# Linear attention on one core: in one slot of each batch ScalarE copies the numerators and the turned output ahead of the attention's output rows instead of behind them

## The chip, the core and the metric

The kernel runs on 1 core of one Trainium2 chip. The metric is the device time of one execution in microseconds (us). Before the change it is 707.77 us, the median of 3 runs (707.38 to 709.08). The engines of the core work side by side: TensorE (PE; its weight loads are PEld), VectorE (DVE), ScalarE (ACT), GpSimd (POOL), and SyncE (SP), which issues DMAs. Each engine takes its own instructions strictly in order; semaphores connect them.

## The reference, cut to what matters

Eight batches of 512 tokens with 128 features go through an AdaLN block: a causal linear attention with 16 heads, then a softmax attention over groups, and a mixture of experts with 8 experts and one chosen for each token. The change lies in the first part:

```python
h = _layernorm(x, axis=-1) * (1 + ca) + sa
# linear attention on h
q = (elu(q) + 1.0 + FEAT_EPS) / sqrt(E);  k = elu(k) + 1.0 + FEAT_EPS
kv_cumsum = cumsum(einsum('blhe,blhf->blhef', k, v), axis=1)
num = einsum('blhe,blhef->blhf', q, kv_cumsum)
den = einsum('blhe,blhe->blh', q, cumsum(k, axis=1))[..., None] + FEAT_EPS
out = (num / den).reshape(B, L, D) @ Wout.T + bout
attn = (out - mu) / sqrt(var + LN_EPS) * gamma + beta      # the output rows, normalised
x = x + ga * attn
h = _layernorm(x, axis=-1) * (1 + cb) + sb                 # input of the second part
```

## The kernel before, in words

All five engines run one program written out by hand. The linear attention is a pipeline over steps: `for s in STEPS` (from -3 to 8), and in each step eight slots `for d in range(NL)`. In step s the attention of batch s is computed. A batch has four chunks of 128 tokens and each chunk two units of eight heads, so slot d handles unit g = 8s + d, chunk d // 2. Beside it the same step prepares batch s + 2 (functions with a_ in the name: layer norm, projections, features, and three bf16 parts of the features) and works up batches s - 1 to s - 3 (functions with c_: normalise, residual, second layer norm, softmax projections). From step 6 on there is no batch left to prepare.

The attention of a unit goes round four engines:

- TensorE: `before` (L925, the state of the chunks ahead, into the bank b_nm; it waits until ScalarE has emptied that bank), `turn` (L946, transposes of the numerators of the chunk before), `products` (L910, for the next unit; it waits for VectorE's mask of this unit), `numerators` (L936, into b_nm). In even slots also `turn_back` (L952), in odd ones `project` (L958).
- VectorE: `masked` (L1402, two instructions, PSUM times the causal mask), `normalise` (L1417, L1419), `output` (L1427).
- ScalarE: in even slots `numerators_out` (L1914, the bank b_nm to SBUF, 512 columns) and `output_out` (L1918, the turned output, 128 columns).

When the four chunks of a batch are done, its output rows are normalised: `c_stats(s - 1, 0)` on VectorE in slot 4 (L1431 to L1438), `c_rstd` (L649, L650, L653) and `x_shifted` (L657) on GpSimd in slot 4, `c_normed(s - 1, 0)` on ScalarE (L1969, four instructions of 128 columns, one for each chunk, into c_t), and `x_ready(s - 1)` on GpSimd in slot 5: L662 multiplies c_t by the gate, L665 adds it to x. Both read two SBUF tensors of 512 fp32 columns. `c_stats(s - 2, 1)` of the next step needs their result.

In slots 5 and 6 VectorE also makes the features of batch s + 2: `a_feature` (L1546, two SBUF inputs, once in slot 5 and once in slot 6) and `a_rest` (L1552, two SBUF inputs; the first in slot 6 waits for ScalarE's `a_first_part`, L1952). GpSimd's `a_last_part` (L644) follows them. On ScalarE slot 6 also has `c_h_out(s - 2)` (L1978, the transposed rows of the second layer norm), for which TensorE's `c_query` (L1017) in slot 7 waits.

Program text sets the order on every engine; there is no scheduler.

Of the kernel before, what the change touches and what calls it, by code (L numbers as in the profile page):

```python
# [199 lines left out]
def wait(eng, sem, value):  # L200

    if isinstance(value, int) and value <= 0:
        return
    eng.wait_ge(sem, value)
# [27 lines left out]
def carve(space):  # L232


    at = [0]
    names = "abcd"

    def piece(shape, dt=F32, parts=P):
        n = math.prod(shape) // (2 if dt is BF16 else 1)
        ap = space[0:parts, at[0]:at[0] + n]  # L240
        at[0] += n
        if dt is BF16:
            ap = ap.bitcast(BF16)
        axes = names[0:len(shape)]
        sizes = {axis: size for axis, size in zip(axes, shape)}
        return ap.rearrange("p (" + " ".join(axes) + ") -> p " + " ".join(axes), **sizes) if len(shape) > 1 else ap

    return piece


def program(nc, k):
# [21 lines left out]
    with ExitStack() as ctx, ExitStack() as early:  # L273
# [37 lines left out]
        d = carve(k.a_space)  # L311
# [58 lines left out]
        def has(b):  # L370
            return 0 <= b < B

        def chunk(q):
            return 0 <= q < B * C
# [7 lines left out]
        def tile(a, b, c):  # L382
            if a is k.h_all:
                return k.h_tiles[:, b * C + c, 0:D]
            return a[:, b * W + c * D:b * W + (c + 1) * D]
# [108 lines left out]
        with nc.Block() as block:  # L494
# [1415 lines left out]
            def _(act):  # L1910
                def numerators_out(q):
                    act.wait_ge(s_nm, 2 * q + 2)
                    wait(act, s_tr, q - 1)
                    act.activation(nt[:, q % 2, :], b_nm[:], ACT.Identity, bias=k.den_eps[:]).then_inc(s_nt, 1)  # L1914

                def output_out(q):
                    act.wait_ge(s_ot, q + 1)
                    act.activation(ot[:, q % 2, :], b_oy[:, 0:P], ACT.Copy).then_inc(s_oc, 1)  # L1918

                def values(b):  # L1920
                    act.wait_ge(a_s_vc, b + 1)
                    if b == 0:
                        act.wait_ge(w_s_f, 3)
                    wait(act, s_nm, NL * (b - 1))
                    act.activation(vp[b % 2][:, :, :, 0:E], of(k.v_all, b).rearrange("p (c h e) -> p c h e", c=C, h=H),
                                   ACT.Copy).then_inc(s_vp, 1)

                def a_normed(a):
                    act.wait_ge(a_s_nb, a + 1)
                    wait(act, a_s_tr, a)  # L1930
                    for c in range(C):
                        last = act.activation(a_xn[:, c * D:(c + 1) * D], tile(k.x_all, a, c), ACT.Identity,
                                              bias=a_nb[:, c:c + 1], scale=a_rs[:, c:c + 1])
                    last.then_inc(a_s_xn, 1)

                def a_h_out(a):
                    act.wait_ge(a_s_tr, a + 1)
                    if a == 0:
                        act.wait_ge(w_s_v, QUERY)
                    act.activation(a_ht[:], b_x[:], ACT.Identity, bias=k.sat[:, a:a + 1], scale=k.ca1t[:, a:a + 1]  # L1940
                                   ).then_inc(a_s_ht, 1)
# [12 lines left out]
                def a_second_part(a, z):  # L1954
                    act.wait_ge(a_s_r1, 2 * a + z + 1)
                    act.activation(a_parts[:, 3 * z + 1, :], a_r1[:, z, :], ACT.Copy).then_inc(a_s_p2, 1)  # L1956

                def a_key_out(a):
                    act.wait_ge(a_s_kt, a + 1)
                    act.activation(h_of(a), k.tiles(b_y[:], C), ACT.Copy).then_inc(a_s_kc, 1)  # L1960

                def c_normed(b, m):
                    act.wait_ge(c_s_nb[m], b + 1)
                    if m == 0:
                        wait(act, c_s_h, b)
                    elif m == 2:
                        wait(act, c_s_tr, b)
                    for c in range(C):
                        last = act.activation((c_xn if m == 2 else c_t)[:, c * D:(c + 1) * D],  # L1969
                                              tile((k.v_all, k.x_all, k.h_all)[m], b, c), ACT.Identity,  # L1970
                                              bias=c_nb[:, m, c:c + 1], scale=c_rs[:, m, c:c + 1])
                    last.then_inc(c_s_n[m], 1)
# [8 lines left out]
                def c_first_part(b, z):  # L1981
                    act.wait_ge(c_s_pj, 2 * b + z + 1)
                    wait(act, c_s_ps, 16 * b)
                    act.activation(c_parts[:, 3 * z, :], (b_x, b_z)[z][:], ACT.Copy).then_inc(c_s_p1, 1)

                def c_second_part(b, z):
                    act.wait_ge(c_s_r1, 2 * b + z + 1)
                    act.activation(c_parts[:, 3 * z + 1, :], c_r1[:, z, :], ACT.Copy).then_inc(c_s_p2, 1)
# [67 lines left out]
                for s in STEPS:  # L2056
                    for d in range(NL):
                        g = s * NL + d
                        if d % 2 == 0 and chunk((g - 2) // 2):
                            numerators_out((g - 2) // 2)  # L2060
                        if d % 2 == 0 and chunk((g - 4) // 2):
                            output_out((g - 4) // 2)
                        if d == 0:
                            if has(s + 1):
                                a_second_part(s + 1, 1)
                            if s == 0:
                                a_key_out(s + 1)
                            if s == -1:
                                act.wait_ge(w_s_m, 2)
                                act.activation(mrow[:, 2, :], k.bank[3][0:B, 2 * D:3 * D], ACT.Copy, bias=1.0  # L2070
                                               ).then_inc(w_s_mr, 1)
                                act.activation(mrow[:, 3, :], k.bank[3][0:B, D:2 * D], ACT.Copy).then_inc(w_s_mr, 1)
                                a_normed(s + 2)
                                a_key_out(s + 1)
                            if has(s - 3):
                                c_first_part(s - 3, 1)
                        if d == 1:
                            if has(s + 1):
                                values(s + 1)
                            if has(s - 2):  # L2080
                                c_normed(s - 2, 1)
                            if has(s - 3):
                                c_second_part(s - 3, 0)
                        if d == 2:
                            if has(s + 2):
                                a_h_out(s + 2)
                            if has(s - 3):
                                c_values_out(s - 3)
                                c_second_part(s - 3, 1)
                        if d == 4:  # L2090
                            if has(s + 2):
                                a_exp(s + 2, 0)
                                a_exp(s + 2, 1)
                            if has(s - 2):
                                c_normed(s - 2, 2)
                        if d == 5 and s == B:
                            maxima_out(0, b_num)
                        if d == 5 and has(s - 1):
                            c_normed(s - 1, 0)
                        if d == 6:  # L2100
                            if has(s - 2):
                                c_h_out(s - 2)
                            if has(s + 2):
                                a_first_part(s + 2, 0)
                        if d == 7:
                            if has(s + 2):
                                a_first_part(s + 2, 1)
                                a_second_part(s + 2, 0)
                            if has(s + 3) and s != -2:
                                a_normed(s + 3)  # L2110
                            if has(s + 2) and s > -1:
                                a_key_out(s + 2)
                            if has(s - 2) and s < B:
                                c_first_part(s - 2, 0)
# [105 lines left out]
```

## Time and profile before

| what | value |
|---|---|
| time, 3 runs | 707.77 us median (707.38 to 709.08) |
| profiled execution: span from the first to the last instruction | 705.1 us |
| its time outside the span, against the median of the runs | 2.7 us |
| TensorE busy | 629.5 us (89%) |
| VectorE busy | 609.4 us (86%) |
| ScalarE busy | 494.0 us (70%) |
| GpSimd busy | 418.5 us (59%) |
| chain of waits, by engine | PE 51%, DVE 20%, ACT 17%, issue 6%, POOL 3% |
| mean granted clock of TensorE | 0.970 |

The profiled execution is known by its span; its own full time isn't listed apart from the three runs, so the distance between span and time is taken against their median. Busy shares are means over stages with different limits: the linear attention fills about the first 250 us, the softmax attention and the experts the rest. A row of a timeline reads: start, duration, engine, line, operation, output<-input, columns, count, and in brackets how long the engine sat idle before it and what ended that.

### The profile page before, as it was taken

To read this page: it belongs to the slowest core of one execution; us is meant where nothing else is said; L and a number is where in the kernel's file an instruction comes from. 1 tells how busy PE (TensorE), PEld (TensorE's weight loads), DVE (VectorE), ACT (ScalarE), POOL (GpSimd) and SP (SyncE) were. 2 spreads that over 40 slices of the span, in tenths; PEclk is the share of its full clock that TensorE was granted. 3 is DMA by queue.
4 is the path that set the end of the run, shared out by engine and by line. 5 is a ranking of instruction groups with operands and counts; after the bars stand their busy time and mean duration, and the time that the engine had idled before them with its cause. 6 is when DMAs were issued, how large, how long until landed. Compare 5 with 4: busy or idle time off the path is not lost.

```text
span 705.1 us, 16639 instructions
## 1 busy us (share of the span) xinstructions
PE 629.5 (89%) x5448; PEld 323.9 (46%) x5448; DVE 609.4 (86%) x1566; ACT 494.0 (70%) x1007; POOL 418.5 (59%) x931
## 2 busy tenths in 40 slices
PE   4599689889887798899999999999999999899994
PEld 2366566666555322222323323233333322498994
DVE  6878999998977898899999999999999995686552
ACT  3634656766645347888888888888898889855662
POOL 6212666575656457135676787887777872566553
PEclk9899999999999959999999999999999999999997
DMA  6664133243263313016430120302103001456600
GB/s 180 176 215 122 49 111 108 97 158 106 92 203 98 89 46 110 26 54 202 121 91 2 58 69 13 113 25 87 39 19 109 25 12 35 138 171 175 173 31 12
DMA packets 42900, 66.26 MB, mean 94 GB/s; under 512 B 7948, under 2 KB 36335, under 8 KB 39808
## 3 DMA queue, kind: packets, MB, share of 16 engines
q1 hardware_dynamic: 39232, 56.73, 26.8%
q0 software_dynamic: 3296, 8.41, 3.3%
q8 instruction: 45, 0.74, 0.5%
q14 instruction: 39, 0.32, 0.2%
q10 hardware_dynamic: 288, 0.07, 0.0%
HBM read 41.64 MB, written 22.26 MB: 91 GB/s over the span
## 4 chain that ended last, share of the span: by engine, by line
PE 51%; DVE 20%; ACT 17%; issue 6%; POOL 3%; DMA 1%; SPq 1%; ACTq 0%; POOLq 0%; DVEq 0%
PE bank L1081 11%; ACT arena L2000 10%; PE pair L1070 7%; DVE arena L1569 6%; PE bank L1042 6%; PE pair L1331 4%; DVE arena L1402 4%; PE pair L1340 2%; PE bank L1340 2%; DVE arena L1431 2%; PE bank L1092 2%; PE bank L936 2%; ACT arena L1969 2%; PE bank L925 2%; DVE arena L1552 1%
## 5 line engine op out<-in xcount | busy, mean ns | idle before, releaser
L2000 ACT ACTIVATE arena<-pair 128x512 f32<-128x512 f32 x506 | 278.1, 602 | 50.5 <-PE pair L1070 48.6
L1569 DVE TENSOR_REDUCE arena<-bank 128x1 f32<-128x512 f32 x388 | 251.3, 682 | 7.5 <-PE bank L1042 6.5
L1070 PE MATMUL pair<-q_stack,k_stack 64*128 64x512 bf16 x506 | 158.0, 386 | 5.9 <-ACT arena L2000 5.3
L1042 PE MATMUL bank<-k_stack,q_stack 63*128 63x512 bf16 x388 | 137.4, 395 | 8.6 <-DVE arena L1569 4.8
L1081 PE MATMUL bank<-arena,values 128*9 128x512 f32 x1024 | 134.7, 598 | 1.6 <-ACT arena L2000 1.5
L1402 DVE TENSOR_TENSOR arena<-bank,cst 128x512 f32<-128x512 f32 x128 | 82.1, 682 | 15.6 <-PE bank L910 15.1
L1569 DVE TENSOR_REDUCE arena<-pair 128x1 f32<-128x512 f32 x124 | 84.3, 680 | 1.5 <-PE pair L1042 1.1
L1042 PEld LDWEIGHTS bank<-k_stack,q_stack 63*128 63x128 bf16 x388 | 33.3, 93 | 109.6 <-DVE arena L1569 24.9
L715 POOL TENSOR_TENSOR arena<-arena 128x32 f32<-128x32 f32 (+6 forms) x312 | 68.8, 220 | 24.4
L1070 PEld LDWEIGHTS pair<-q_stack,k_stack 64*128 64x128 bf16 x506 | 40.6, 93 | 48.6 <-ACT arena L2000 26.4
L1914 ACT ACTIVATE arena<-bank,den_eps 128x512 f32<-128x512 f32 x32 | 21.7, 677 | 41.2 <-PE bank L936 41.2
L1042 PE MATMUL pair<-k_stack,q_stack 63*128 63x512 bf16 x124 | 49.0, 395 | 0.5 <-ACT v_all L2025 0.3
L878 POOL DMA_INDIRECT out_dram<-arena,e_token_u x32 | 31.2, 976 | 23.1 <-DVE arena L1861 19.6
L649 POOL TENSOR_SCALAR arena<-arena 128x4 f32<-128x4 f32 x24 | 5.5, 230 | 64.4 <-DVE arena L1438 64.2
L925 PE MATMUL bank<-fq_all,arena 128*128 128x128 f32 x192 | 30.9, 283 | 14.1 <-ACT arena L1914 14.1
L751 POOL DMA_INDIRECT token_rows<-arena,d_places_u x32 | 33.7, 1053 | 15.4 <-POOL d_places_u L739 5.2
L2136 ACT ACTIVATE fq_all<-pair 128x512 f32<-128x512 f32 x39 | 23.3, 596 | 26.6 <-PE pair L1331 26.6
L1331 PE MATMUL pair<-q_stack,h_all 128*128 128x128 f32 x312 | 41.5, 276 | 0.0
L936 PE MATMUL bank<-arena,values 128*9 128x128 f32 x1024 | 40.8, 278 | 0.0
L1331 PEld LDWEIGHTS pair<-q_stack,h_all 128*128 128x128 f32 x312 | 38.0, 192 | 0.0
L925 PEld LDWEIGHTS bank<-fq_all,arena 128*128 128x128 f32 x192 | 26.1, 191 | 23.0 <-ACT arena L1914 17.3
L644 POOL TENSOR_TENSOR arena<-arena 128x512 bf16<-128x512 f32 x15 | 17.4, 1162 | 30.4 <-ACT arena L1956 30.4
(301 smaller groups left out, 1262.0 us busy)
## 6 DMA issues: line engine op xcount, KB each, us to landing
softmax_parts<-arena SPq DMA_DIRECT2D x8, 768.0 KB
q_stack<-softmax_parts SPq DMA_DIRECT2D x48, 128.0 KB, 2.9
k_stack<-softmax_parts SPq DMA_DIRECT2D x48, 128.0 KB, 3.0
linear_parts<-arena SPq DMA_DIRECT2D x7, 768.0 KB, 3.7
q_stack<-linear_parts SPq DMA_DIRECT2D x42, 128.0 KB, 2.9
k_stack<-linear_parts SPq DMA_DIRECT2D x42, 128.0 KB, 2.9
arena<-in_L_ffn_w_dram SPq DMA_DIRECT2D x16, 256.0 KB, 4.5
v_all<-token_rows SPq DMA_DIRECT2D x20, 192.5 KB, 2.7
```

Source lines behind the costliest of these rows:

```text
L715: done(pool.tensor_tensor(half[:, 0:w], src[:, 0:w], src[:, w:2 * w], ALU.add))
L751: pool.indirect_dma_start(k.rows_dram, bass.IndirectOffsetOnAxis(ap=k.pos_u[:, f:f + 1], axis=0), row_slot(f), None, bounds_check=NE * REG ...
L878: pool.indirect_dma_start(out_rows, bass.IndirectOffsetOnAxis(ap=token_u[:, j:j + 1], axis=0), yo[j], None, bounds_check=T * P - 1, oob_is ...
L925: pe.matmul(b_nm[:, cols], spad[u][:, c - 1, cols], k.fq_all[:, b * L + c * P:b * L + (c + 1) * P], start=(gg == 0), stop=False, skip_grou ...
L936: last = pe.matmul(b_nm[VW * j:VW * j + E + 1, cols], vp[u][:, c, GH * (2 * hp + gg) + j, :], b_am[:, g % 2, gg, j, :], start=(c == 0), st ...
L1042: pe.matmul(bank[:], qs[b % 2][rows, slot, qt * P:(qt + 1) * P], ks[b % 2][rows, slot, :], start=True, stop=True).then_inc(d_s_m, 1)
L1070: pe.matmul(score_bank(s)[:], ks[u][rows, 2 * g + x, kt * P:(kt + 1) * P], qs[u][rows, 2 * g + x, :], start=True, stop=True).then_inc(d_s_ ...
L1081: last = pe.matmul(b_num[VW * q:VW * q + E + 1, :], vp[b % 2][:, kt, GH * g + q, :], pt[:, kt % 2, q % 2, q // 2, :], start=(kt == 0), sto ...
L1331: last = pe.matmul(b_up[j % 2][:, c * P:(c + 1) * P], w1c[j % R4][:, c * P:(c + 1) * P], xt[j % R4], start=True, stop=True)
L1402: dve.tensor_tensor(b_am[:, g % 2, gg], k.tiles(b_at[gg][:], GH), k.rep(k.causal, GH), ALU.mult).then_inc(s_am, 1)
L1569: dve.reduce_max(mx[:, m % 2, col:col + 1], bank[:], AX).then_inc(d_s_mr, 1)
L2000: act.activation(pt[:, kt % 2, x, half, :], score_bank(s)[:], ACT.Exp, scale=SCALE).then_inc(d_s_e, 1)
```

## The change

The call of `c_normed(s - 1, 0)` on ScalarE moves from the end of slot 5 to slot 6, behind `numerators_out` and `output_out` of that slot and ahead of everything else in it:

```diff
@@ -2060,6 +2060,8 @@
                             numerators_out((g - 2) // 2)
                         if d % 2 == 0 and chunk((g - 4) // 2):
                             output_out((g - 4) // 2)
+                        if d == 6 and has(s - 1):
+                            c_normed(s - 1, 0)
                         if d == 0:
                             if has(s + 1):
                                 a_second_part(s + 1, 1)
@@ -2095,8 +2097,6 @@
                                 c_normed(s - 2, 2)
                         if d == 5 and s == B:
                             maxima_out(0, b_num)
-                        if d == 5 and has(s - 1):
-                            c_normed(s - 1, 0)
                         if d == 6:
                             if has(s - 2):
                                 c_h_out(s - 2)
```

ScalarE's queue in slots 5 and 6 of a step that still prepares a batch (steps 2 to 5; in step 1 the rows ahead and L1978 are missing). L1969 over v_all are the output rows, L1914 the numerators, L1918 the turned output:

```order
 L1969 ACTIVATE arena<-h_all,arena 128x128 [waits c_transposed,c_shift2]
 L1969 ACTIVATE arena<-h_all,arena 128x128 x3
+L1914 ACTIVATE arena<-bank,den_eps 128x512 [waits b_turned,b_numerators]
+L1918 ACTIVATE arena<-pair 128x128 [waits b_output_turned]
 L1969 ACTIVATE arena<-v_all,arena 128x128 [waits c_h_ready,c_shift0]
 L1969 ACTIVATE arena<-v_all,arena 128x128 x3
-L1914 ACTIVATE arena<-bank,den_eps 128x512 [waits b_turned,b_numerators]
-L1918 ACTIVATE arena<-pair 128x128 [waits b_output_turned]
 L1978 ACTIVATE arena<-pair,lnw 128x512 [waits c_transposed]
 L1952 ACTIVATE arena<-fq_all 128x512 [waits a_parts_stored,a_features]
```

The four instructions over v_all and the pair behind them have changed places; what follows (L1978, L1952) stays behind both.

The same place in steps 6 and 7, where nothing is prepared any more:

```order
+L1914 ACTIVATE arena<-bank,den_eps 128x512 [waits b_turned,b_numerators]
+L1918 ACTIVATE arena<-pair 128x128 [waits b_output_turned]
 L1969 ACTIVATE arena<-v_all,arena 128x128 [waits c_h_ready,c_shift0]
 L1969 ACTIVATE arena<-v_all,arena 128x128 x3
-L1914 ACTIVATE arena<-bank,den_eps 128x512 [waits b_turned,b_numerators]
-L1918 ACTIVATE arena<-pair 128x128 [waits b_output_turned]
 L1978 ACTIVATE arena<-pair,lnw 128x512 [waits c_transposed]
 L1984 ACTIVATE arena<-pair 128x512 [waits c_parts_stored,c_projected]
```

Here L1978 is followed by the copy of TensorE's projection (L1984). The queues of the other engines hold the same instructions in the same order as before.

## Rows read from the trace of the kernel before

**Rows 1.** Windows: two steps; busy us of each engine, granted clock, DMA
```profile
151.50:178.10 26.60, 23.55 (x296) 16.68 (x300) 23.78 (x72) 17.70 (x39) 15.71 (x20) 1.00 0.39 119
...
203.20:226.80 23.60, 18.46 (x263) 12.79 (x264) 17.93 (x61) 11.51 (x27) 12.83 (x16) 1.00 0.41 127
```

**Rows 2.** Chain of waits in step 5: start, length on the chain, what
```profile
181.89 1.77 DVE arena L1552
183.66 1.20 DVE arena L1402 x2
```

**Rows 3.** Timeline of VectorE, step 5, slots 5 and 6
```profile
180.09 1.28 DVE L1402 TENSOR_TENSOR arena<-bank,cst 128x512 f32<-128x512 f32 x2
181.29 0.68 DVE L1546 SCALAR_TENSOR_TENSOR arena<-arena 128x512 f32<-128x512 f32 x1
```

**Rows 4.** Timeline of TensorE, step 5
```profile
172.12 0.62 PE L936 MATMUL bank<-arena,values 128*9 128x128 f32 x16
...
178.01 0.62 PE L936 MATMUL bank<-arena,values 128*9 128x128 f32 x16
...
180.40 0.71 PE L925 MATMUL bank<-fq_all,arena 128*128 128x128 f32 x4 [1.51 <-ACT arena L1914]
...
181.49 0.40 PE L910 MATMUL bank<-q_stack,k_stack 63*128 63x128 bf16 x8
```

**Rows 5.** Timeline of ScalarE, step 5
```profile
172.81 0.69 ACT L1914 ACTIVATE arena<-bank,den_eps 128x512 f32<-128x512 f32 x1 [3.79 <-PE bank L936]
...
173.56 1.27 ACT L1945 ACTIVATE arena<-pair,bq 128x512 f32<-128x512 f32 x2
...
178.13 1.65 ACT L1969 ACTIVATE arena<-v_all,arena 128x128 f32<-128x128 f32 x4 [1.78 <-POOL arena L653]
179.69 0.67 ACT L1914 ACTIVATE arena<-bank,den_eps 128x512 f32<-128x512 f32 x1
...
181.08 0.62 ACT L1952 ACTIVATE arena<-fq_all 128x512 bf16<-128x512 f32 x1
```

**Rows 6.** Line L1552, all steps: ns min/median/max, first and last start
```profile
L1552 DVE TENSOR_TENSOR arena<-fq_all,arena x8: 681/1762/1769, 18.1 to 181.9; 128x512 f32<-128x512 f32 x8
L1552 DVE TENSOR_TENSOR arena<-arena x8: 679/682/707, 18.8 to 185.5; 128x512 f32<-128x512 f32 x8
```

**Rows 7.** Timeline of GpSimd, step 5
```profile
179.86 1.45 POOL L662 TENSOR_TENSOR arena<-arena 128x512 f32<-128x512 f32 x1 [0.54 <-ACT arena L1969]
181.45 1.66 POOL L665 TENSOR_TENSOR x_all<-x_all,arena 128x512 f32<-128x512 f32 x1
184.40 1.16 POOL L644 TENSOR_TENSOR arena<-arena 128x512 bf16<-128x512 f32 x1 [1.29 <-ACT arena L1956]
```

**Rows 8.** Timelines of GpSimd and VectorE, step 3, where they meet
```profile
113.93 1.27 POOL L672 TENSOR_TENSOR h_all<-arena 128x512 f32<-128x512 f32 x1
114.07 1.17 DVE L1438 TENSOR_SCALAR arena<-arena 128x4 f32<-128x4 f32 x1
```

**Rows 9.** Timelines of ScalarE, TensorE and VectorE, step 6 and end of step 7
```profile
203.22 1.65 ACT L1969 ACTIVATE arena<-v_all,arena 128x128 f32<-128x128 f32 x4 [1.15 <-POOL arena L653]
203.49 0.62 PE L936 MATMUL bank<-arena,values 128*9 128x128 f32 x16
204.78 0.67 ACT L1914 ACTIVATE arena<-bank,den_eps 128x512 f32<-128x512 f32 x1
205.50 0.77 ACT L1978 ACTIVATE arena<-pair,lnw 128x512 f32<-128x512 f32 x1
207.02 1.29 DVE L1402 TENSOR_TENSOR arena<-bank,cst 128x512 f32<-128x512 f32 x2 [2.13 <-PE bank L910]
207.79 1.02 PE L1017 MATMUL pair<-arena,wsm 128*128 128x512 f32 x2
209.63 1.29 DVE L1402 TENSOR_TENSOR arena<-bank,cst 128x512 f32<-128x512 f32 x2 [0.63 <-PE bank L910]
...
235.29 2.48 DVE L1569 TENSOR_REDUCE arena<-bank 128x1 f32<-128x512 f32 x4 [0.15 <-PE bank L1042]
```

## The prediction

> **What bounds the kernel now.** The edit acts only in the linear attention stage, so I read the stage before the engine totals. The windows come first [rows 1]. In the step from 151.5 to 178.1 us VectorE is busy 23.78 of 26.60 us, ScalarE 17.70, GpSimd 15.71; in the step from 203.2 to 226.8 us, which no longer prepares a later batch, VectorE is busy only 17.93 of 23.60 us. So two kinds of step are to be expected, one held by VectorE and one held by something else. In the code c_normed(s - 1, 0) exists in steps s = 1 to 8. Steps 1 to 5 are of the first kind, 6 and 7 of the second, and in step 8 no numerators are copied in slot 6, so nothing moves there.
>
> Next comes the chain of waits in step 5: it runs through VectorE, through L1552 (1.77 us) and straight on into L1402 [rows 2]. The VectorE timeline there shows no idle in front of its instructions [rows 3]. The TensorE timeline does show idle: L925 at 180.40 waited 1.51 us for ScalarE's L1914, the copy of the numerators [rows 4]. That is the wait that the edit shortens. ScalarE's own timeline says why: c_normed (L1969, four instructions, 1.65 us) started at 178.13 after waiting for GpSimd, and L1914 stood behind it until 179.69 [rows 5].
>
> Last, the length of L1552. Two instructions of each step that prepares a batch stand on that line, both 512 columns of fp32. The second takes 0.68 us (median 682 ns), the first 1.76 (median of 8, least 0.68) [rows 6]. The long one began at 181.89 while GpSimd's L665 (x_ready, SBUF operands) ran from 181.45 to 183.11, and ended 0.55 us behind it, at 183.66 [rows 2, 7]. L665 itself began 0.16 us behind VectorE's L1546 and took 1.66 us, against 1.27 of L672, the same shape with no such neighbour [rows 3, 7, 8]. So here a VectorE and a GpSimd operation over SBUF don't run side by side: the one that starts second waits until about 0.13 us before the recorded end of the first (183.66 - 0.68 = 182.98 against 183.11; 183.11 - 1.27 = 181.84 against 181.97). What GpSimd does in x_ready therefore sets VectorE's time, and the edit moves x_ready.
>
> **The change, steps 1 to 5.** Nothing is added or taken away; on ScalarE two groups change places. The numbers are those of step 5; the other four repeat its pattern.
> Numerators: L936 starts at 178.01. Where ScalarE is free, L1914 starts 0.69 us behind it (172.12 to 172.81) [rows 4, 5]. So it starts at 178.70 in place of 179.69, 0.99 us earlier.
> TensorE: L925 and L946 come up to 0.99 us earlier, but then L910 (products of the next slot) needs VectorE's L1402 to be done, which is at 180.09 + 1.28 = 181.37; before, L910 started at 181.49 [rows 3, 4]. The gain there is about 0.05 us, and VectorE doesn't wait for it. Value of the shorter wait in these steps: nothing, since VectorE's queue covers it.
> Row normalisation: from an idle start L1914 and L1918 take 0.75 us (172.81 to 173.56) [rows 5]. c_normed starts at 178.70 + 0.75 = 179.45 in place of 178.13 and ends at 181.10. L662 starts 0.08 us behind its end (178.13 + 1.65 to 179.86) [rows 5, 7], so at 181.18 in place of 179.86. L657 on GpSimd, ahead of it, stays where it was.
> Behind it ScalarE reaches L1952 2.95 us after the first of the three groups starts, as before (178.13 to 181.08) [rows 5]: at about 181.66, end 182.3. L1552 waits for that, but would by the next step not start before it anyway.
> VectorE: its second L1546 starts at 181.29 and nothing has moved it [rows 3]. GpSimd's L662 now starts 0.11 us ahead of it. The nearest row: L672 started at 113.93, L1438 on VectorE at 114.07, 0.14 us behind, and L1438 took 1.17 us, until 115.24, where L672 ended at 115.20 [rows 8]. So L1546 waits: it works from 181.18 + 1.27 - 0.13 = 182.32 in place of 181.29, 1.03 us late. L665 is issued 0.14 us behind L662's end (1.45 us from 179.86, then 181.45) [rows 7], at 182.59, and waits for L1546 to let go at about 182.87; L1552 follows at 182.92 and finds L665 there, exactly as it does now (let go at 181.84, L665 waiting, L1552 at 181.89 second). L1552 so keeps its 1.77 us and ends at 184.69 in place of 183.66.
> The cost is 1.03 us in a step, and it is on the path, since L1402 follows without idle [rows 2]. It isn't recovered later: what the next step waits for (ScalarE's L1956, GpSimd's L644, the products) starts from VectorE's results. The bounds of this term are 0 (VectorE first) and 1.77 - 0.68 = 1.09 us, the whole wait that the trace shows for one such meeting. I take 1.03: 5 x 1.03 = +5.1 us.
>
> The Trainium skill, "SBUF — State Buffer", section "Who interferes with whom", says that whoever issues first has the ports shared by VectorE and GpSimd for a whole instruction and that the other blocks fully; rows 6 to 8 agree with it (1.77 against 0.68 us), and by it the sum is the same +5.1. Against the argument speaks its page "Perfetto Trace Analysis", section "GPSIMD Engine Instruction", which calls GpSimd's recorded spans unreliable: if so, 0.11 us says little on who is first, and the sum could as well be that of the first rival below. No row here decides it; the lead of 0.14 us in rows 8 is the best there is.
>
> **Steps 6 and 7.** Here VectorE waits: 2.13 us in front of L1402 at 207.02 and 0.63 in front of the one at 209.63, both for TensorE's L910, and that stands behind L1914 [rows 9]. L1914 could start at 203.49 + 0.69 = 204.18 in place of 204.78, 0.60 us earlier, and L1402 with it (206.42). But c_h_out (L1978) now starts 2.28 us behind 204.18 plus 0.02, at 206.48 (203.22 to 205.50 is the span of the three groups) and ends at 207.25, and TensorE's L1017 waits for it: with 0.05 us for the signal and 0.1 for the weights it starts at 207.4 in place of 207.79 [rows 9]. So 0.4 us are left, for L910 and the L1402 behind. GpSimd's L662 and L665 meet no VectorE operation over two SBUF operands there. At the end of step 7 VectorE still waits 0.15 us for TensorE (L1042, at 235.29) [rows 9], so the 0.4 passes on. Between 0 and 0.6, I take 0.4: 2 x 0.4 = -0.8 us.
>
> Sum: +5.1 - 0.8 = +4.3 us on the span of 705.1, so 709.4. The runs have a median of 707.8, 2.7 above that span; with the same distance the forecast is 712.1 us.
>
> **Rivals.**
> First, the meeting goes the other way: L1546 gets the ports in front of L662 (or L1552 in front of L665). For it speaks that the lead is 0.11 us and that VectorE's queue runs without a gap, where L1438 stood alone; against it rows 8. Then L662 ends at 183.1 as L665 does today, L1552 keeps its 1.77 us, and L665 runs to 184.52 beside L1402. L644, before at 184.40, comes up to 0.1 later and can hold up the second L1552 at 185.5 by 0.05 [rows 6, 7]. 5 x 0.05 - 0.8 = -0.5: 707.2 us. This is the case on the other side, not slower; it decides from the point where L662 starts later than L1546, which 0.12 us more on ScalarE or 0.1 on GpSimd would bring.
> Second, TensorE is the bound and its 1.51 us wait [rows 4] costs in full: 5 x 0.99 + 2 x 0.60 = 6.2 us less, 701.6 us. Against it speaks that VectorE has no idle there; for it only that TensorE's wait is the longest idle in the step.
> Third, the steps differ: in some GpSimd is first and in some VectorE. Each costs 1.0 or nothing, so 708 to 711 us. Against it: the offsets repeat within 0.02 us from step to step.
>
> **How the numbers follow.** Forecast 55 in 100 (712.1 us, own range 711.3 to 713), first rival 28, second 6, third 11. A measurement of this kernel can tell about 0.3%, 2.1 us, from no change: under 705.6 is faster, over 709.9 slower. Slower: 55 + 6 of the third = 61. Same: 28 + 4 = 32. Faster: 6 and 1 for a small shift beyond the first rival, 7. The range 706.5 to 713.3 leaves out the second rival and a little on both sides of the others.
>
> **What would show it.** Right: the second L1546 of steps 1 to 5 at 1.7 us (now 0.68) with L662 starting about 0.1 in front of it, L1552 still 1.77, L925's wait for L1914 in slot 6 down from 1.51 to about 0.5, steps 1 to 5 each 1.0 longer, steps 6 and 7 each 0.4 shorter. Wrong: L1546 at 0.68 in all steps (first rival), or steps 1 to 5 shorter than before (second). The prediction fails above all if L662 starts behind L1546 or the lead doesn't count.

## The result, and the profile after

The changed kernel takes 712.27 us (median of 4 runs, 711.14 to 712.51), the kernel before 708.03 us (4 runs, 707.38 to 709.08). The ratio is 1.0051, with a 95% interval of 1.004 to 1.0063: slower by half a per cent, 4.2 us. On three other chips the kernel before takes some 15 us more; on one of them the two were measured again, and the ratio is 1.0066 (1.005 to 1.0083).

The span of the profiled execution grew from 705.1 to 710.6 us. The timeline of VectorE in step 5 of the kernel after (start, duration, then as in the rows of before):

```profile
183.52 1.28 DVE L1402 TENSOR_TENSOR arena<-bank,cst 128x512 f32<-128x512 f32 x2
184.72 1.70 DVE L1546 SCALAR_TENSOR_TENSOR arena<-arena 128x512 f32<-128x512 f32 x1
186.34 1.76 DVE L1552 TENSOR_TENSOR arena<-fq_all,arena 128x512 f32<-128x512 f32 x1
188.03 1.28 DVE L1402 TENSOR_TENSOR arena<-bank,cst 128x512 f32<-128x512 f32 x2
```

and of GpSimd:

```profile
184.60 1.27 POOL L662 TENSOR_TENSOR arena<-arena 128x512 f32<-128x512 f32 x1 [1.85 <-ACT arena L1969]
186.01 1.54 POOL L665 TENSOR_TENSOR x_all<-x_all,arena 128x512 f32<-128x512 f32 x1
188.84 1.16 POOL L644 TENSOR_TENSOR arena<-arena 128x512 bf16<-128x512 f32 x1 [1.29 <-ACT arena L1956]
```

Against [rows 3, 7]: the second L1546 takes 1.70 us instead of 0.68, and it begins 0.12 us behind L662, which before began 1.43 us ahead of it and had let go. L1552 keeps its 1.76 us behind L665. The same in all five steps; the line as a whole:

```profile
L1546 DVE SCALAR_TENSOR_TENSOR fq_all<-arena,fq_all x8: 681/682/684, 17.3 to 182.9; 128x512 f32<-128x512 f32 x8
L1546 DVE SCALAR_TENSOR_TENSOR arena<-arena x8: 681/1694/1702, 17.9 to 184.7; 128x512 f32<-128x512 f32 x8
```

ScalarE and TensorE in the same place:

```profile
182.14 0.69 ACT L1914 ACTIVATE arena<-bank,den_eps 128x512 f32<-128x512 f32 x1 [2.36 <-PE bank L936]
182.72 0.27 ACT L1918 ACTIVATE arena<-pair 128x128 f32<-128x128 f32 x1
182.88 1.64 ACT L1969 ACTIVATE arena<-v_all,arena 128x128 f32<-128x128 f32 x4
```

```profile
182.88 0.71 PE L925 MATMUL bank<-fq_all,arena 128*128 128x128 f32 x4 [0.55 <-ACT arena L1914]
183.43 0.60 PE L946 MATMUL bank<-cst,arena 128*128 128x128 f32 x4
184.86 0.40 PE L910 MATMUL bank<-q_stack,k_stack 63*128 63x128 bf16 x8 [0.84 <-DVE arena L1402]
```

TensorE's wait for the numerators fell from 1.51 [rows 4] to 0.55 us, as the change intends. Two instructions later L910 waits 0.84 us for VectorE, and L910 of the next slot, behind the late L1402, another 1.02 us (at 189.45): nothing of the shorter wait reaches the end. The chain of waits shows the new length in VectorE's part:

```profile
183.60 1.20 DVE arena L1402 x2
184.81 0.97 DVE arena L1546
185.77 0.57 issue
186.34 1.76 DVE arena L1552
188.10 1.20 DVE arena L1402 x2
```

Measured from one L657 to the next (its start, once in a step), the whole difference of the two spans can be laid out, before against after:

| stretch | before, us | after, us | difference |
|---|---|---|---|
| up to step 1 | 72.41 | 71.70 | -0.71 |
| step 1 | 25.47 | 27.00 | +1.53 |
| step 2 | 26.57 | 27.60 | +1.03 |
| step 3 | 27.01 | 27.58 | +0.57 |
| step 4 | 26.59 | 27.60 | +1.01 |
| step 5 | 25.09 | 26.10 | +1.01 |
| step 6 | 23.76 | 24.26 | +0.50 |
| step 7 | 24.14 | 24.26 | +0.12 |
| the rest | 454.06 | 454.50 | +0.44 |
| sum | 705.1 | 710.6 | +5.5 |

The windows of step 4, and of step 6, of the kernel after (columns as in rows 1):

```profile
153.88:181.48 27.60, 23.82 (x298) 16.70 (x300) 24.80 (x72) 17.68 (x39) 15.38 (x20) 1.00 0.37 119
207.58:231.84 24.26, 20.21 (x267) 13.95 (x268) 18.10 (x62) 11.50 (x26) 12.87 (x17) 0.93 0.40 127
```

Here a step runs from its slot 4 (L657) into slot 4 of the next. Against [rows 1] VectorE is 1.02 us busier in step 4 with the same 72 instructions; that is waiting, recorded as work. In step 6 the granted clock of TensorE was 0.93 instead of 1.00, which is told of below.

### The profile page after: what moved, and what is told of

The parts are those of the page before. It is cut to its first block, busy times and chain, and to the rows that moved or that the text cites. A ratio compares the mean times of both kernels' runs of the same rounds, so it can differ in the third digit from the quotient of the medians.

```text
span 710.6 us, 16639 instructions
## 1 busy us (share of the span) xinstructions
PE 631.8 (89%) x5448; PEld 324.4 (46%) x5448; DVE 615.7 (87%) x1566; ACT 493.6 (69%) x1007; POOL 415.7 (58%) x931
## 4 chain that ended last, share of the span: by engine, by line
DVE 41%; PE 34%; ACT 11%; issue 6%; SPq 5%; DMA 2%; POOL 2%; ACTq 0%; POOLq 0%; DVEq 0%
DVE arena L1569 26%; PE bank L1081 5%; ACT arena L2000 5%; PE pair L1331 4%; DVE arena L1402 3%; PE pair L1070 3%; PE bank L1042 3%; PE pair L1340 2%; PE bank L1340 2%; DVE arena L1431 2%; PE bank L936 2%; DVE arena L1552 2%; ACT arena L1969 2%; PE bank L925 1%; PE bank L910 1%
## 5 line engine op out<-in xcount | busy, mean ns | idle before, releaser
L1402 DVE TENSOR_TENSOR arena<-bank,cst 128x512 f32<-128x512 f32 x128 | 82.2, 683 | 15.4 <-PE bank L910 15.1
L1914 ACT ACTIVATE arena<-bank,den_eps 128x512 f32<-128x512 f32 x32 | 21.8, 682 | 59.6 <-PE bank L936 59.5
L936 PE MATMUL bank<-arena,values 128*9 128x128 f32 x1024 | 40.8, 278 | 0.0
L910 PE MATMUL bank<-q_stack,k_stack 63*128 63x128 bf16 x512 | 25.9, 221 | 15.9 <-DVE arena L1402 14.6
L925 PE MATMUL bank<-fq_all,arena 128*128 128x128 f32 x192 | 31.1, 285 | 8.1 <-ACT arena L1914 7.5
L644 POOL TENSOR_TENSOR arena<-arena 128x512 bf16<-128x512 f32 x15 | 17.4, 1158 | 29.6 <-ACT arena L1956 29.6
```

What stands on the lines that cost most here:

```text
L910: last = pe.matmul(b_at[gg][:, j * P:(j + 1) * P], ks[u][rows, LIN_SLOT[p], c * P:(c + 1) * P], qs[u][rows, LIN_SLOT[p], c * P:(c + 1) * P ...
L925: pe.matmul(b_nm[:, cols], spad[u][:, c - 1, cols], k.fq_all[:, b * L + c * P:b * L + (c + 1) * P], start=(gg == 0), stop=False, skip_grou ...
L936: last = pe.matmul(b_nm[VW * j:VW * j + E + 1, cols], vp[u][:, c, GH * (2 * hp + gg) + j, :], b_am[:, g % 2, gg, j, :], start=(c == 0), st ...
L1402: dve.tensor_tensor(b_am[:, g % 2, gg], k.tiles(b_at[gg][:], GH), k.rep(k.causal, GH), ALU.mult).then_inc(s_am, 1)
```

## The experiments

In the kernels with added lines the line numbers in the rows are shifted. In pause1, pause3 and pause8, L1546, L1552, L662, L665 and L644 are called L1549, L1555, L665, L668 and L645, and L1952 and L1969 are L1955 and L1972; in the kernels add_later, L1546, L1552 and L665 are L1553, L1559 and L668, and L1402, L910, L925, L936, L946 and L1914 are each seven higher. The text keeps the old names. Times are compared as ratios with the kernel before, run in turn on the same chip; lengths of steps come from the profiled execution. These chips take 722.5 to 723.9 us for the kernel before, almost all of the difference behind the stage in question: steps 1 to 5 have the same lengths there to 0.01 us where the clock is the same (late_only).

### The new order only in steps 6 and 7, and only in steps 1 to 5

```diff
-                        if d == 6 and has(s - 1):
+                        if d == 6 and has(s - 1) and s > 5:
                             c_normed(s - 1, 0)
...
+                        if d == 5 and has(s - 1) and not (s > 5):
+                            c_normed(s - 1, 0)
```

> The new ScalarE order only in steps 6 and 7, the old one in steps 1 to 5. Theory (the cost is GpSimd's L662 meeting VectorE's second L1546 in steps 1 to 5; steps 6 and 7 gain): 0.8 us under the kernel before, so about 707.2; the second L1546 takes 0.68 us in every step, and L1402 in slot 7 of steps 6 and 7 waits about 1.55 us instead of 2.13. Rival (it is the late output rows themselves that cost, in every step in which they come later): about 1 to 2 us above the kernel before.

Measured: ratio 0.9982 (0.9969 to 0.9995), -1.3 us (-0.4 to -2.2). The second L1546 is 0.68 us in every step; L1402 in slot 7 of steps 6 and 7 waits 1.55 instead of 2.13 us, the next 0.81 instead of 0.63. The time is as the theory has it. In its profiled execution step 6 is nevertheless 24.17 us long, at a clock of 0.93, against 23.76 at 1.00.

The other half is the same edit with s <= 5:

> The new ScalarE order only in steps 1 to 5, the old one in steps 6 and 7. Theory: 5 x 1.0 = 5 us above the kernel before, about 713.1, which is 0.8 above the changed kernel; the second L1546 takes 1.7 us in steps 1 to 5. Rival (steps 6 and 7 carry part of the cost): under 712.

Measured: ratio 1.009 (1.0064 to 1.0116), +6.5 us, more than the 5 forecast and more than the changed kernel. Steps 2 to 5 take 27.61, 27.60, 27.60 and 26.10 us, the lengths of the kernel after; the second L1546 is 1.70 us. Step 1 took 28.04 us at a clock of 0.88, against 25.47 at 1.00 in the kernel before. So steps 1 to 5 carry the whole loss, and the order in steps 6 and 7 is not to blame.

### A pause on GpSimd in front of L662

```diff
                     pool.wait_ge(c_s_n[0], b + 1)
+                    for i in range(3):
+                        pool.memset(k.pause[:, i:i + 1], 0.0)
```

With the changed kernel's order on all other engines; pause1 has one memset, pause8 eight.

> The changed kernel with three more instructions: memsets of one column on GpSimd between its wait for the normalised rows and L662, so that L662 starts some 0.2 to 0.3 us later. Theory (who starts first has the ports): L662 now starts behind the second L1546, which takes 0.68 us again, L662 and L665 shift, and the time falls to that of the first rival of the prediction, about 707.3 us, 5 us faster with more work. Rival (the cost comes from ScalarE's later rows or later L1952, not from who meets whom): 712.3 or a little more.

> The same with one memset. L662 started 0.12 us ahead of L1546 in the changed kernel; one memset shifts it by some 0.05 to 0.15 us. Theory: if it then still leads, 712.3, and if it starts behind, 707.3, so the time is one of the two and not between them. Rival (the two share the ports and each slows in proportion to the overlap): a small change, under 1 us.

Measured: pause3 1.0064 (1.004 to 1.0089), pause1 1.0078 (1.0047 to 1.0109). The expected fall of 5 us in pause3 didn't come, since three memsets moved L662 by only 0.10 us. But that put it on the tie, and one execution shows both outcomes. GpSimd and VectorE of pause3, in step 3 and then in step 4:

```profile
130.35 1.27 POOL L665 TENSOR_TENSOR arena<-arena 128x512 f32<-128x512 f32 x1
...
158.03 1.85 POOL L665 TENSOR_TENSOR arena<-arena 128x512 f32<-128x512 f32 x1
```

```profile
130.38 1.79 DVE L1549 SCALAR_TENSOR_TENSOR arena<-arena 128x512 f32<-128x512 f32 x1
...
158.06 0.68 DVE L1549 SCALAR_TENSOR_TENSOR arena<-arena 128x512 f32<-128x512 f32 x1
159.08 1.35 DVE L1555 TENSOR_TENSOR arena<-fq_all,arena 128x512 f32<-128x512 f32 x1 [0.34 <-ACT arena L1955]
```

In both steps GpSimd is recorded 0.03 us ahead. In step 3 it takes 1.27 us and VectorE 1.79; in step 4 VectorE takes 0.68 and GpSimd 1.85. Step 3 lasts 27.68 us, step 4 26.90, with the same instructions and the same clock of 1.00. L1546 never took anything between the two, which speaks against shared, slowed-down access. In pause1 the lead was 0.08 to 0.09 us and VectorE lost in all five steps (1.73 to 1.74 us), as expected for a lead that is kept.

> The changed kernel as it is, to stand on the same chip as the two below. From step 1 to step 8 (start of L657) some 5 to 6 us more than the kernel before; steps 1 to 5 at 27.6 us against 26.6, the second L1546 at 1.70 us with L662 0.12 us in front.

> The changed kernel with eight memsets ahead of L662 where three had moved it by 0.10 us, just to the tie. L662 is then issued 0.1 to 0.2 us behind the second L1546. Theory (the first to start has the ports; the loser waits): L1546 0.68 us in all five steps, L662 1.8 to 2.0, L1552 about 1.35, and 1.0 for the second L1552, which meets L644; each of steps 1 to 5 some 0.7 us shorter than in the changed kernel and 0.3 longer than in the kernel before, so 3.5 us under the changed kernel on the same chip. Rival (ScalarE's later rows cost by themselves): no more than 1 us under the changed kernel.

Measured: after_again 1.0066 (1.005 to 1.0083), pause8 1.0008 (0.9993 to 1.0022), on one chip; in medians 727.14 and 722.87 us. Sixty-four instructions more (eight in each of the eight batches) make the changed kernel 4.3 us faster (3.5 forecast). VectorE and GpSimd of pause8 in step 5:

```profile
181.34 0.68 DVE L1549 SCALAR_TENSOR_TENSOR arena<-arena 128x512 f32<-128x512 f32 x1
182.36 1.34 DVE L1555 TENSOR_TENSOR arena<-fq_all,arena 128x512 f32<-128x512 f32 x1 [0.34 <-ACT arena L1955]
...
185.50 1.00 DVE L1555 TENSOR_TENSOR arena<-arena 128x512 f32<-128x512 f32 x1
```

```profile
181.20 0.30 POOL L664 MEMSET pause<- 128x1 f32 x8 [1.83 <-ACT arena L1972]
181.45 1.70 POOL L665 TENSOR_TENSOR arena<-arena 128x512 f32<-128x512 f32 x1
183.29 1.54 POOL L668 TENSOR_TENSOR x_all<-x_all,arena 128x512 f32<-128x512 f32 x1
184.79 1.16 POOL L645 TENSOR_TENSOR arena<-arena 128x512 bf16<-128x512 f32 x1
```

L662 is issued 0.11 us behind L1546 and it is GpSimd that waits. L1552 ends 2.36 us behind the start of L1546, as in the kernel before (183.66 - 181.29 = 2.37): part of that is now a wait of 0.34 us for ScalarE's late L1952. Step 5 is 25.40 us, 0.70 less than in the changed kernel and 0.31 more than before (step 4: 26.88, 0.72 less and 0.29 more), and that 0.3 is the second L1552, which takes 1.00 us because GpSimd, running later, is at L644 when it starts. So this is the first rival of the prediction made real, with its price: it is no gain either.

### The same meeting without the change on ScalarE

In the kernel before, GpSimd's L657 of steps 1 to 5 is moved behind the wait for the normalised rows, which brings L662 to the same instant as in the changed kernel:

```diff
                     pool.wait_ge(c_s_n[0], b + 1)
+                    if 1 <= b + 1 <= 5:
+                        x_shifted(b)
                     pool.tensor_tensor(t, t, row(k.G_OF, b), ALU.mult).then_inc(c_s_g, 1)
...
-                            x_shifted(s - 1)
+                            if s > 5:
+                                x_shifted(s - 1)
```

> The kernel before, ScalarE's order unchanged, with GpSimd's L657 of steps 1 to 5 moved from ahead of its wait for the normalised rows to behind it, ahead of L662. L662 then starts about 1.3 to 1.45 us later, at 181.2 to 181.3 in step 5, within 0.1 us of the second L1546 at 181.29. Theory: with L662 first, L1546 takes 1.7 us and the time is 5 us above the kernel before although ScalarE does the same at the same times, 713; with L1546 first, L1552 still meets L662 or L665 and the time is 708 to 709. Rival (ScalarE's order costs): 708 in either case, with L1546 at 0.68 us.

Measured: ratio 1.0047 (1.0029 to 1.0066), +3.4 us (2.1 to 4.8), under the 5 forecast, with ScalarE's old order. In steps 2 to 5 L662 led by 0.02 to 0.03 us and the second L1546 took 1.79 to 1.82 us, in step 1 it led by 0.02 and lost (L1546 0.68, L662 1.83). Four lost meetings at 1.1 us would be 4.4, inside the interval. From one L1546 to the next steps 2 and 3 take 27.7 us. The cost follows GpSimd's timing and not ScalarE's order.

### The other meeting taken away

L665 (x_added) of steps 1 to 5 goes behind L644 in slot 0 of the next step:

```diff
                             a_last_part(s + 1, 0)
+                        if d == 0 and has(s - 2) and s <= 6:
+                            x_added(s - 2)
...
                             x_ready(s - 1)
+                            if s > 5:
+                                x_added(s - 1)
```

> The kernel before with GpSimd's L665 (the second half of x_ready) of steps 1 to 5 moved behind L644 of the next step's slot 0; ScalarE's order is the old one. Theory: L665 no longer meets the first L1552, which falls from 1.76 to 0.68 us, and nothing else takes its place: 5 x 1.09 = 5.4 us less, 702.6. If TensorE then becomes the bound in part, 703 to 705. Rival (L1552 is long for another reason, such as its wait for ScalarE's part): no change, 708.

> The same move of L665 in the changed kernel. Theory: L662 still meets the second L1546 (1.7 us), L665 no longer meets L1552 (0.68 us): each meeting costs by itself, so 5.4 us under the changed kernel, about 706.9, and 4.3 above the kernel before with the same move. Rival (the two meetings cost once together): no more than the kernel before with the move, about 703.

> The kernel before with L665 moved as before and the new ScalarE order in steps 6 and 7 alone. Theory: both gains add, 702.6 - 0.8 = 701.8 us, faster than both kernels of the case. Rival (they don't add): 702.6 or more.

Measured: add_later 0.9953 (0.993 to 0.9976), -3.4 us; add_later_after 0.9978 (0.9965 to 0.9992), -1.6 us, which is 5.3 us under the changed kernel by its first ratio (1.0051) and 6.4 by its second (1.0066), where 5.4 was forecast; add_later_late 0.9937 (0.9914 to 0.9959), -4.6 us, the lowest ratio of the case and under both kernels of the case. The old order gained less than the theory had: add_later 3.4 us where 5.4 was forecast, add_later_late 4.6 where 6.2 was, and the two ScalarE orders lie 1.8 us apart instead of 4.3. The first L1552 is 0.68 to 0.69 us in every step of all three. In add_later_after L1546 stays at 1.70, and steps 2 to 5 take 26.52, 26.51, 26.53 and 25.02 us, 1.08 less than in the kernel after: each meeting costs by itself, and in steps 2 to 5 of the changed kernel the whole of the second is to be had back. In the old order of ScalarE it is not, and add_later_late shows why. Its windows of steps 3 and 4:

```profile
124.09:151.09 27.00, 24.78 (x298) 17.64 (x299) 24.84 (x82) 18.02 (x39) 17.15 (x22) 0.94 0.35 114
151.09:176.59 25.50, 23.28 (x298) 16.64 (x299) 22.69 (x72) 17.67 (x39) 15.72 (x19) 1.00 0.39 120
```

Step 4, at full clock, is 25.50 us, 1.09 under the kernel before. Step 3, at 0.94, is 27.00. TensorE there, and VectorE behind it:

```profile
126.45 0.71 PE L932 MATMUL bank<-fq_all,arena 128*128 128x128 f32 x4 [1.50 <-ACT arena L1921]
127.00 0.96 PE L953 MATMUL bank<-cst,arena 128*128 128x128 f32 x4
127.89 0.61 PE L917 MATMUL bank<-q_stack,k_stack 63*128 63x128 bf16 x8
128.43 1.04 PE L943 MATMUL bank<-arena,values 128*9 128x128 f32 x16
```

```profile
130.44 0.68 DVE L1559 TENSOR_TENSOR arena<-arena 128x512 f32<-128x512 f32 x1
132.53 1.29 DVE L1409 TENSOR_TENSOR arena<-bank,cst 128x512 f32<-128x512 f32 x2 [1.41 <-PE bank L917]
```

The second of these matmul groups takes 0.96 us where it takes 0.60 at full clock, the fourth 1.04 instead of 0.62, and VectorE, now quicker, waits 1.41 us for TensorE. The kernel before has the same length in its own step at 0.94 (step 3, 27.01 us, with both meetings as they were): in a step with such a stretch TensorE holds the chain, and a shorter L1552 gives nothing. The twelve runs of add_later spread from 715.48 to 722.98 us, and mostly with the clock: the four under 718 us have a mean of 0.960 or 0.961, the four at 0.952 or less all take over 721 us (but the longest has 0.957). Its profiled execution, at 722.76, is one of the long ones.

A last version made L665 wait for the second L1552 as well, since in one step of add_later_late it had been issued ahead of it and made it 0.9 us longer (in step 2, which at a clock of 0.94 took 27.00 us like step 3):

```diff
+                            pool.wait_ge(a_s_r1, 2 * (s + 1) + 2)
                             x_added(s - 2)
```

> The kernel before with L665 of steps 1 to 5 behind L644 and, new, behind a wait for the second L1552, and the new ScalarE order in steps 6 and 7 alone. The run without that wait gained 1.09 us in two of the five steps and lost it again in others, where L665 was issued ahead of the second L1552 (1.58 us) or TensorE's clock was low. Theory: both L1552 at 0.68 us in all five steps, ratio to the kernel before 0.990 to 0.993, under both kernels of the case. Rival (TensorE is the bound as soon as L1552 is short): the same as without the wait, 0.994 or above.

Measured: 0.9941 (0.9917 to 0.9964), no better than without the wait, so the expectation missed and its rival holds. Both L1552 are 0.68 us in all steps, but steps 1 to 3 ran at a clock of 0.87, 0.94 and 0.94 and took 26.24, 27.01 and 27.01 us; steps 4 and 5, at 1.00, took 25.50 and 24.01. In this execution (720.13 us, above the median of 718.77) the clock is what is left once the two L1552 are short.

## Why the prediction was right, and where it wasn't

The bound was right: in steps 1 to 5 VectorE holds the chain, and TensorE's shorter wait (1.51 to 0.55 us) shortened no step there by itself: L910 waits for VectorE behind it.

The meeting was right in place and size. Against VectorE's queue L1914 started 0.98 us earlier than in the old order, L662 1.31 us later, 0.12 us in front of L1546 (forecast 0.11), which took 1.02 us longer (forecast 1.03). Steps 1 to 5 grew by 5.15 us (forecast 5.1), though not each alike: step 1 by 1.53, with a clock of 0.94 and L1402 waiting 0.64 us for TensorE, and step 3 by 0.57, because the low-clock stretch was gone that in the kernel before had made L1402 wait 0.35 us there and the step 0.4 us longer than its neighbours. Neither was forecast, and that the two cancel (+0.5 and -0.45 beside five times 1.02) is luck. Early_only and late_only put the loss into these steps, pause3 and pause8 into who is first, shift_between into GpSimd's timing and not ScalarE's order.

The bounds of the term held (0 to 1.09), but its upper end was not the highest possible: at the tie VectorE waited 1.10 to 1.14 us.

The late steps came out otherwise in the profile. The forecast was -0.8 us for both; there they are +0.50 and +0.12 (in after_again, on another chip, 0.00 and -0.10). The waits changed as worked out (2.13 to 1.55, 0.63 to 0.81, -0.40 together in each), but TensorE's clock was lower (0.93 instead of 1.00 in step 6, 0.78 instead of 0.84 in step 7), and in step 6 one L1402 waited 3.24 us, where the same one waited 2.33 before. TensorE and VectorE of the kernel after:

```profile
221.44 0.99 PE L925 MATMUL bank<-fq_all,arena 128*128 128x128 f32 x4 [2.02 <-ACT arena L1914]
222.23 1.06 PE L946 MATMUL bank<-cst,arena 128*128 128x128 f32 x4
```

```profile
223.87 1.29 DVE L1402 TENSOR_TENSOR arena<-bank,cst 128x512 f32<-128x512 f32 x2 [3.24 <-PE bank L910]
```

The two matmul groups take 0.99 and 1.06 us; at full clock they take 0.71 and 0.60 (182.88 and 183.43 above). In pause1, with step 6 at 1.00, the step was 23.47, 0.29 under the kernel before, and over the runs late_only gained 1.3 us. So the mechanism is there: 0.29 us in that step, and 0.65 a step by the runs of late_only (0.2 to 1.1 by its interval), which holds the forecast of 0.4. The profiled execution of after doesn't show it, and what the clock does in these steps was no term of the forecast.

The sum came out at 712.1 against 712.27, closer than its parts. The forecast span was 709.4 and the measured one 710.6, 1.2 more: 0.7 less up to step 1, 1.4 more in steps 6 and 7, 0.4 more in the rest. Against it stands that I took 2.7 us as the distance between span and time, where the profiled execution of after took 712.41, 1.8 over its span: so the profiled execution of before was probably a short one (705.1 + 1.8 = 706.9 is under the lowest of its runs), not one further outside its span. Two errors of about 1 us with opposite signs: that the sum comes within 0.2 us is luck. What the experiments confirm are two of its terms, the 5.1 us of the meetings and a gain in the late steps.

The first rival had its price wrong. I gave it 0.05 us a step through L644; pause8 shows 0.3 (1.00 instead of 0.68 for the second L1552), since L665 was held up behind L1552 and L644 with it, and step 4 of pause3, where VectorE won by itself, the same (26.90 us). Its time would have been about that of the kernel before (pause8: 1.0008), not 0.5 us less.

The doubt drawn from the page "Perfetto Trace Analysis" of the Trainium skill, that GpSimd's recorded spans are no ground for 0.11 us, wasn't borne out here: leads of 0.08 to 0.09 us (pause1) and of 0.12 us (after) decided alike in 5 of 5 steps each, and only at 0.02 to 0.03 did the outcome vary. The rule of "SBUF — State Buffer", section "Who interferes with whom", that the one issued first blocks the other fully, agrees with every meeting of L662 and the second L1546 (L1546 takes 0.68 us or 1.69 to 1.82, and where it takes 0.68, L662 takes 1.70 to 1.85 instead of 1.27); at a recorded lead of 0.02 to 0.03 us the trace doesn't tell which of the two was issued first.

## What to carry to other kernels

A wait that is shortened on an engine off the chain gives nothing by itself; look instead at what the moved work does to the start times of everything it releases. Where VectorE and GpSimd both work over SBUF, compare start times to a tenth of a microsecond: moving one by a little can cost the other a whole instruction, and a GpSimd operation is best placed beside VectorE's PSUM work (L1402 took 1.28 us with L662 beside it almost all the way, [rows 3, 7], and 1.27 to 1.29 wherever it ran in this stage). A duration that is longer than that of the same shape elsewhere can be a wait in disguise, and taking it away (here L665, -3.4 us) was worth more than shortening the visible idle (late_only, -1.3 us).

## What the runs showed of the hardware that I had not expected

- The tie is narrow. With GpSimd recorded 0.02 to 0.03 us ahead VectorE lost seven of ten meetings (pause3, shift_between); at 0.08 and more it lost all 25 (after, after_again, early_only, pause1, add_later_after). When GpSimd was issued 0.11 us behind (pause8), VectorE won in all five steps, and 0.04 to 0.06 us were enough: in the three kernels add_later the second L1552 started that much ahead of L665 in twelve steps and took 0.68 us in each, and L665 1.75 to 1.78.
- TensorE's stretches at half its clock (1.2 instead of 2.4 GHz) moved with the order of ScalarE. The old order has an idle of 1.5 us on TensorE in slot 6 of steps 1 to 5; the new one has 0.55 there and then up to 0.84 and 1.02 in front of the next two L910 (steps 2 to 5). In steps 2 to 5 the windows of the seven kernels with the new order there (28 steps) all show a granted clock of 1.00; in the six with the old order (24 steps) eleven show 0.93 or 0.94, and in the rows above the stretch begins right behind the 1.5 us. In the window of step 6, where both orders have an idle of about 2 us before L925 in slot 2 of step 7, the clock was 0.93 in ten of thirteen kernels, 1.00 in the kernel before. In step 1, though, six of the seven with the new order show 0.88 to 0.94 and three of the six with the old, so the idle in slot 6 can't be all of it. The meeting itself may have a part in that: in step 1 of after, after_again, early_only, pause1 and pause3, where the lost meetings make L1402 late, L910 of slot 7 waits 1.87 us for it, and the slow matmul groups begin 2.0 to 2.6 us behind that; in pause8, where L1546 is short, the same wait is 1.31 us and the clock 1.00. In add_later_after the stretch begins before slot 7. No run tested the idle apart, so its effect on the clock isn't shown. If it holds for steps 2 to 5, the new order does earn something at TensorE: with L1552's meeting gone, it loses 1.02 us a step to L1546 and gets part of it back by clock, and that would be why add_later_after and add_later are only 1.8 us apart.
